# Attention 0 of a Flamingo-style block: batch 6's value bias moves from four ScalarE operations into its residual rows on GpSimd, the bias row and the rows are loaded earlier, and two of four weight units are loaded after the last K group

## What is computed

```python
x = x + jnp.tanh(g_xattn[0]) * _L0_xattn_ref(_layernorm(x, axis=-1), ctx_1024, ctx_1024, mask_BxS2_ik0,
                                             L0_xattn_Wq, L0_xattn_bq, L0_xattn_Wk, L0_xattn_bk, L0_xattn_Wv, L0_xattn_bv)
x = x + jnp.tanh(g_ffn[0]) * _L0_ffn_ref(_layernorm(x, axis=-1), ...)
# inside _L0_xattn_ref:
v = _heads(x_v @ Wv.T + bv)
p = jax.nn.softmax(scores, axis=-1)
h = jnp.einsum('bhqk,bhkw->bhqw', p, v)
```

## Time and profile before

| what | value |
|---|---|
| median of 3 runs | 1576.35 us (1574.77 to 1576.37) |
| the profiled execution's own time | 1575.78 us |
| its span, first to last instruction | 1573.8 us |
| PE busy / DVE / ACT / POOL | 99% / 65% / 62% / 27% of the span |
| granted TensorE clock | 1.00 |

### The profile page before, as it was taken

How to read it: one execution, slowest core, us unless ns; L and a number is a source line. 1 busy time by engine, 2 the same in 40 slices (tenths; PEclk the granted TensorE clock), 3 DMA queues, 4 the chain that set the end, 5 groups by cost and what they waited for, 6 DMA issues and landing times.

```text
span 1573.8 us, 25733 instructions
## 1 busy us (share of the span) xinstructions
PE 1562.3 (99%) x9306; PEld 1428.5 (91%) x9306; DVE 1025.0 (65%) x1814; ACT 971.6 (62%) x2014; POOL 425.1 (27%) x570
## 2 busy tenths in 40 slices
PE   9999999999999999999999999999999999999999
PEld 7999899999989999999999998889999989988765
DVE  6577887787786562123644425647777777778987
ACT  5676777677775455444544435447677767767676
POOL 4221221222145222222322222311211121123741
PEclk9999999999999999999999999999999999999999
DMA  8766767687582226554375642576676677668500
GB/s 250 186 168 169 198 179 198 161 204 183 137 221 97 95 81 201 183 181 164 105 233 190 217 164 90 183 184 185 156 193 174 169 188 180 173 142 223 193 13 31
DMA packets 149974, 261.29 MB, mean 166 GB/s; under 512 B 41136, under 2 KB 94000, under 8 KB 149709
## 3 DMA queue, kind: packets, MB, share of 16 engines
q1 hardware_dynamic: 149505, 259.24, 58.7%
q10 hardware_dynamic: 332, 0.23, 0.1%
HBM read 191.01 MB, written 58.57 MB: 159 GB/s over the span
## 4 chain that ended last, share of the span: by engine, by line
PE 94%; DVE 3%; ACT 2%; issue 1%; DMA 0%; ACTq 0%; DVEq 0%
PE ps L1235 33%; PE ps L862 16%; PE ps L866 14%; PE ps L962 8%; PE ps L940 8%; PE ps L1169 2%; PE ps L1031 2%; PE ps L882 2%; PE ps L929 2%; PE ps L924 2%; PE ps L1186 1%; PE ps L927 1%; PE ps L928 1%; ACT P L1953 1%; PE ps L1080 1%
## 5 line engine op out<-in xcount | busy, mean ns | idle before, releaser
L1235 PE MATMUL ps<-ah_f,wh_f 128*128 128x400 f32 x1288 | 442.0, 344 | 0.0
L1235 PE MATMUL ps<-al_f,wh_f 128*128 128x400 f32 x1288 | 441.3, 343 | 0.0
L2317 POOL TENSOR_TENSOR cxl<-raw,cxh 128x384 fp32r<-128x384 f32 (+1 forms) x112 | 105.6, 964 | 558.2 <-ACT cxh L1895 558.2
L1817 DVE TENSOR_TENSOR wl_f<-raw_f,wh_f 128x1024 fp32r<-128x1024 f32 x85 | 103.7, 1223 | 232.1 <-POOL wh_f L2307 232.1
L1384 DVE TENSOR_REDUCE nmax<-ps 100x1 f32<-100x722 f32 x256 | 220.8, 903 | 33.1 <-PE ps L928 29.5
L1235 PEld LDWEIGHTS ps<-al_f,wh_f 128*128 128x128 f32 x1288 | 242.2, 188 | 0.0
L1235 PEld LDWEIGHTS ps<-ah_f,wh_f 128*128 128x128 f32 x1288 | 241.9, 188 | 0.1
L1953 ACT ACTIVATE P<-ps,nmax 100x722 f32<-100x722 f32 x256 | 220.0, 862 | 27.6 <-DVE nmax L1384 27.4
L1965 ACT ACTIVATE PT<-ps 128x400 fp32r<-128x400 f32 x384 | 165.9, 505 | 70.5 <-PE ps L940 69.4
L2235 ACT ACTIVATE raw_f<-wl_f 128x1024 f32<-128x1024 f32 x88 | 93.5, 1062 | 174.9 <-DVE wl_f L1817 174.9
L1390 DVE TENSOR_TENSOR PT<-ps,PT 128x400 fp32r<-128x400 f32 x384 | 196.4, 567 | 3.2
(11 more groups left out here) (227 smaller groups left out, 2667.5 us busy)
## 6 DMA issues: line engine op xcount, KB each, us to landing
KS<-kd SPq DMA_DIRECT2D x192, 361.0 KB
raw_f<-in_h SPq DMA_DIRECT2D x64, 512.0 KB, 4.2
raw_f<-in_gud SPq DMA_DIRECT2D x48, 512.0 KB, 4.4
raw<-in_ctx SPq DMA_DIRECT2D x64, 192.0 KB, 3.5
raw_f<-in_w SPq DMA_DIRECT2D x24, 512.0 KB, 3.6
kd<-ksh SPq DMA_DIRECT2D x60, 192.0 KB, 2.1
kd<-ksl SPq DMA_DIRECT2D x60, 192.0 KB, 2.4
raw<-in_ctx SPq DMA_DIRECT2D x64, 169.0 KB, 4.2
```

What stands on the lines that cost most here:

```text
L1235: return e.matmul(o, p, q, start=start, stop=stop)
L1817: e.tensor_tensor(wl[:, z, :], raw[:, r, :], raw32(wh[:, z, :]), ALU.subtract).then_inc(v_ul, 1)
L2317: e.tensor_tensor(m.cx[1][:, k, off:off + n], m.raw[:, k, off:off + n], raw32(m.cx[0][:, k, off:off + n]), ALU.subtract).then_inc(g_cx, 1)
```

## The change

In attention 0 batch 6 no longer gets its bias from ACT. Its rows in x0 get the gated bias row on POOL in pair 57, DVE's `add_out(6)` waits for that, and PE's `turn_out(6)` waits for the scaled output instead of the biased one. The bias row is loaded at the end of pair 56 instead of in pair 58, batch 6's rows in pair 57 instead of 59. Two of the four weight units are issued behind the last K group's loads, in pair 58. The multiplication of the row by the gate now stands in pair 57, so that only the addition to x7 is left behind the loop. Numbers in waits follow from that (a_fin counts four fewer).

```diff
@@ SP
-                    if L == 0 and p == 3 and b:
+                    if L == 0 and b and i == (8 * b + 3 if b < B - 1 else 57):
                         load_x0(b - 1)
@@ SP
                         w.wait_ge(g_cx, 56)
-                        for u in range(4):
+                        for u in range(2):
                             fetch(("unit", u))
                     if L == 0 and i == 58:
+                        for u in range(2, 4):
+                            fetch(("unit", u))
+                    if L == 0 and i == 56:
                         w.wait_ge(d_qs[1], qs_done(L, B - 1))
                         e.dma_start(row, t["bv0"].partition_broadcast(S)).then_inc(d_row, 16)
@@ PE, turn_out
-                    if b < B - 1:
+                    if b < KEPT:
                         w.wait_ge(a_fin, 4 * b + 4)
                     else:
-                        w.wait_ge(v_sc, B)
+                        w.wait_ge(v_sc, b + 1)
@@ DVE, add_out
                     w.wait_ge(p_res, b + 1)
+                    if b >= KEPT:
+                        w.wait_ge(g_row, b - KEPT + 1)
@@ DVE, behind the loop
-                    w.wait_ge(g_row, 1)
                     add_out(B - 1)
@@ ACT, high_out
-                    w.wait_ge(a_fin, 4 * (B - 1 + (ROW0[n] + r - 1) // S + 1))
+                    w.wait_ge(a_fin, 4 * (KEPT + (ROW0[n] + r - 1) // S + 1))
@@ ACT
-                    if scaled_at(i) is not None:
+                    if scaled_at(i) is not None and (L or scaled_at(i) < KEPT):
                         add_bias(scaled_at(i))
@@ POOL, pair 57, behind split_kept(0)
+                    if L == 0 and i == 57:
+                        w.wait_ge(d_row, 16 * 7)
+                        w.wait_ge(a_g, 1)
+                        me.then(e.tensor_scalar(row, row, G["x0"][0:S], None, ALU.mult))
+                        me.settle()
+                        w.wait_ge(d_x, 16 * (KEPT + 1))
+                        e.tensor_tensor(x0, x0, row, ALU.add).then_inc(g_row, 1)
@@ POOL, behind the loop
-                    w.wait_ge(d_row, 16 * 7)
-                    w.wait_ge(a_g, 1)
-                    me.then(e.tensor_scalar(row, row, G["x0"][0:S], None, ALU.mult))
-                    me.settle()
                     w.wait_ge(d_x, 16 * B)
                     e.tensor_tensor(x7, x7, row, ALU.add).then_inc(g_row, 1)
```

## The result

The changed kernel takes 1579.1 us (median of 9 runs, 1578.27 to 1582.21) against 1575.22 us before (9 runs, 1574.56 to 1576.37): ratio 1.0027, 95% interval 1.0018 to 1.0035. The time lies in the forecast's range; its size was twice my +2.0, and the wait that sets it is not the one I named.

A forecast was written before the change was run, and what follows sets the result against it. PE, busy for 99% of the span, bounds the kernel. Terms 0 for ACT, DVE and K and +2.0 for POOL, on 1576.35, gave 1578.3 us; forecast band 1577.3 to 1579.4, 8-in-10 range 1575.9 to 1579.8.

The forecast's parts named there:

- "The same": Whole kernel: a time within 0.2%, 3.2 us, of the kernel before, which measurement can't tell from no change; chance 0.84.
- ACT, 0.24 us and not 1.07: Removing ACT's bias additions lets the transposed weights' copy start 0.24 us sooner, not 1.07; covered by the stall, 0 in sum.
- The 0.55 us: Delay of ACT's copy behind PE's transposes where ACT really waits (476.71 to 477.26), used to place the copy at 472.93.
- The queue in front of the row: Older loads hold back the early-issued row until 458.85; it lands at 461.2, the rows at 462.3, unit 0 at 463.6.
- POOL 2.9 us late: POOL's added block in pair 57 ends at 464.4, so prepare(0) and all work through pair 62 is 2.9 us late.
- +2.0 for POOL at spread_sums(7): Late POOL ends spread_sums(7) at 486.7 instead of 484.57; PE goes on 2.05 us late, the only nonzero term.
- K group: Last K group: 4.7 us of loads stand ahead instead of 5.2, so it comes 0.5 us sooner or as before; no cost.
- "0 for DVE": DVE's new waits, add_out(6) and add_out(7), cost nothing: POOL is done in time and PE's transpose still decides add_out(7).
- The first (block covered): Rival: POOL's block fits its 6.38 us idle time, leaving ACT's 0.24 us; 1576.1, up to 1577; chance 0.17.
- the second (ACT's link real): Rival: the bias additions were a real link and POOL is covered; -1.07 us, 1575.3; chance 0.04.
- The third: Rival: POOL over 4.1 us late, or K group missing PE on top; place spread_sums(7), 1579.7 or more; chance 0.13.
- the sign of a wrong K term: If PE also waits at L924 in pair 61, the K group is late and its term is wrong.

The follow-up runs named there:

- loads_only: The kernel before with only the change's DMA issues moved, bias left on ACT and the row's multiplication behind the loop: 1579.48 us.
- wide_loads: The changed kernel with the bias row and batch 6's rows loaded over 128 partitions instead of 100: 1579.42 us.
- wide_act: The kernel before with the change's loads moved, row and batch 6's rows over 128 partitions, bias left on ACT: 1575.58 us.
- in_step_quiet: The changed kernel with row loaded in pair 55, multiplied in 56, both loads over 128 partitions, x7's addition held until DVE has normalized batch 6: 1575.82 us.
- units_ahead: The changed kernel with all four weight units issued ahead of the last K group again: 1582.31 us.
- quiet_pool: wide_loads with POOL's addition to x7 held until DVE has normalized batch 6's rows: 1578.01 us.
- x7_last: The changed kernel with POOL's addition to x7 behind the cast of unit 3 instead of ahead of it: 1578.99 us.
- row_idle: The changed kernel with the bias row loaded in pair 55 and multiplied in pair 56, x0's addition staying in pair 57: 1578.88 us.
- pool_later: The changed kernel with POOL's row multiplication and x0 addition moved from pair 57 to behind the spread sums of pair 59: 1583.4 us.
- in_step: The changed kernel with the edits of row_idle, wide_loads and x7_last together: 1577.02 us.

## Why the prediction was right or wrong

Where the loss sits (3.9 us in the medians, 4.2 between the two profiled executions): the loads cost 4.4 us by themselves (loads_only 1579.48) and POOL's work costs 3.8 by itself once the loads are harmless (wide_loads 1579.42 against wide_act 1575.58). In the changed kernel PE is 3.9 us late through the K group before POOL's 3.1 could reach it, which is why it shows about one of them and not the sum. Both prices contain what the clock costs, which not every execution pays: the three executions of loads_only with a mean clock of 1.000 take 1577.08 to 1578.12 us, the seven below it 1579.27 to 1579.79.

That the time fell into the range is partly luck. The forecast of 1578.3 was built on a median before of 1576.35 us from three executions, and nine gave 1575.22; the change cost 3.9 us and not 2.0; and the wait in the sum isn't the one that occurred. "The same" had a chance of 0.84 and a loss of more than 0.2% one of 0.13; at 0.18% to 0.35% the measurement leaves open which of them it is.

- **What bounds the kernel: right.** PE, 99% busy, and only gaps count.
- **ACT, 0.24 us and not 1.07: right.** The copy starts 475.65 - 475.11 = 0.54 us behind PE's transposes, before 473.17 - 472.38 = 0.79: 0.25 us, inside pair 61's delay. The link of the chain was no lever. The 0.55 us came from a place that doesn't show it (at 477.26 ACT had just ended its operation before, and didn't wait for PE), and was right by luck. Where nothing covers it, PE does get the 0.25 us (in_step_quiet).
- **The queue in front of the row: right.** Forecast 461.2 to 461.3 for the multiplication's start; it came at 460.47 + 0.91 = 461.38, released by the row's load. The row was issued 6.3 us sooner than before (454.78 + 0.91 against 461.96) and landed hardly sooner than unit 0 used to. Unit 0 was forecast for 463.6 and released POOL at 463.74 + 0.91 = 464.65.
- **POOL 2.9 us late: right in size (3.1), and the first wait too** (0.7 forecast in pair 60, 0.89 measured). What failed is its place in the sum. "+2.0 for POOL at spread_sums(7)" does not occur in the changed kernel: there the last rx is read without any wait, and the gap before batch_root(6), which was to be gone, is 1.09 us instead of 0.78. In wide_loads, without the K group's delay, the forecast's wait of 1.5 to 1.7 us is there with 1.52. That the size fits so well is chance again: POOL was 2.3 us late there, not 2.9, PE came a little early instead of 0.45 late, and L979 starts 1.5 us later than before (485.74 + 0.52 against 484.75) where the forecast had 2.05.
- **K group: wrong, and this is the step that failed.** I wrote that it "comes 0.5 us sooner, or at worst as before", by adding up bytes at the rate of full-width loads, 2.6 + 2.1 against 5.2. It kept PE until 3.9 us later than before. The 4.7 us were a sum over 16 engines, though I had just noted that the small loads run on about ten. Shown: over 128 partitions the same loads don't make PE wait for the K group (wide_loads against the change), and cost 0.5 us in the medians instead of 4.4 (wide_act against loads_only), and two more full units in front move pair 61 by 0.5 (units_ahead). Why the number of partitions matters, namely that the engines without a share of the small loads run ahead and that units and K pieces then slow each other, is read from the rates and the records of pieces; no run mixes them on purpose.
- **"0 for DVE": wrong by 1.2 us in the operation and 0.8 at PE.** I checked that the row's multiplication leaves POOL earlier and that PE's transpose still decides add_out(7). I didn't ask what would then stand right behind POOL's COPY, beside DVE's normalization. quiet_pool showed it.
- **The clock: missing from the sum.** My terms priced a wait at its length. In the changed kernel the 0.89 us wait cost another 1.34 us on L958 (hidden, as it turned out, in front of the K wait); in wide_loads and quiet_pool it is in the end time. Two quiet_pool runs out of eleven (1576.57 and 1576.93) lie 0.6 us or more below the rest (1577.54 to 1578.66), and they are the two with a mean clock of 1.000, where all others have 0.999: the program is the same, but the clock doesn't fall every time.
- **The rivals.** The first (block covered) and the second (ACT's link real) are out: no version was faster than before. The third named "K's group missing PE at 471.38 on top" among its mishaps, at a place, spread_sums(7), that wasn't it. It deserved to be a rival of its own: the windows left the K group "hardly any slack", and two new loads stood in front of it. What the prediction gave as the sign of a wrong K term, a wait of PE in pair 61, is what came.

## What to carry to other kernels

Two loads of 100 partitions in front of a tight one cost 3.9 us more here than the same loads over 128: price a small load in front by the share of the DMA engines that it uses, not in bytes alone, and try it over all 128 partitions. When an operation leaves a queue, look at what moves up beside the other engines' work, not only at who waits for the queue. A move that takes work off an engine with cover and puts it on one whose lateness reaches PE had 0.25 us to win here and 3.9 to lose, however long the idle gap in front of it looked: ask first what ended that gap.

## What the hardware showed that I had not expected

- Two loads of 100 partitions (0.2 MB each) in front of units and K group brought the rate to 134 to 141 GB/s at full share for 3 us, below both 410 and 194 to 228 GB/s that these reach one after the other. Over 128 partitions it did not happen.
- DVE's 100x512 normalization took 0.79, 1.78 and 2.02 us, each time ending 0.28 us behind one of POOL's operations, and 0.55 us where POOL ran nothing beside it. Why it gets in between a COPY and a TENSOR_SCALAR of POOL but not between a COPY and an addition or a cast stays open.
- The granted clock fell to the lower level behind waits of PE of 0.89 us (changed kernel), 0.73 (x7_last, pair 60), 1.52 (quiet_pool), 2.24 (loads_only) and 3.53 (units_ahead), and did not behind 0.52 and 1.98 (row_idle), 0.77 (the changed kernel, behind the loop), 0.87 (in_step_quiet) or 2.58 (pool_later, pair 61). So the length of a wait alone doesn't tell. Nor does the program: by the mean clock it fell in nine of eleven executions of quiet_pool and in four of eleven of in_step. What else decides was not tried. Where it fell it cost 1.3 us on 18 matmuls (3.23 instead of 1.89 us), more than the wait of 0.89 us in front of them.
